# A hybrid attention layer on one core: other order of the beginning, first group's stack rows written and loaded alone, weights loaded later

## The reference, cut to what matters

```python
x = x + attn_a(layernorm(x))     # differential attention, 16 heads, two softmax maps per head, head size 4
x = x + ffn(layernorm(x))        # 64 experts of 128x64 and 64x128, top 8 chosen per token, plus a shared expert
x = x + attn_b(layernorm(x))     # attention over sums, 16 heads
x = x + ffn(layernorm(x))

# attn_a, x is (2, 1024, 128) float32
qkv = x @ w_qkv.T
q = q.reshape(B, N, 16, 2, 4); k likewise; v = v.reshape(B, N, 16, 8)
a1, a2 = softmax(q1 k1^T / 2) v, softmax(q2 k2^T / 2) v
o = a1 - lam * a2                # then RMS norm per head, weight, projection
```

## Time and profile before

| | |
|---|---|
| median of 3 runs | 1106.67 us (1105.13 to 1108.87) |
| profiled execution | 1106.26 us, its span 1104.3 us |
| PE busy | 1006.7 us (91%) |
| DVE busy | 958.2 us (87%) |
| ACT busy | 891.8 us (81%) |
| POOL busy | 520.5 us (47%) |
| chain that ended last | DVE 58%, PE 25%, ACT 6%, issue 5%, DMA 5% |

### The profile page before, as it was taken

The page is one execution under the profiler, slowest core; times in us unless marked ns, Lnnn a source line. Parts: engine busy times, 40 slices in busy tenths (PEclk is TensorE's granted clock), DMA queues, the critical chain, the costliest instruction groups (busy, mean ns, idle before and its releaser), DMA issues.

```text
span 1104.3 us, 21657 instructions
## 1 busy us (share of the span) xinstructions
PE 1006.7 (91%) x8016; PEld 516.2 (47%) x8016; DVE 958.2 (87%) x1170; ACT 891.8 (81%) x1466; POOL 520.5 (47%) x909
## 2 busy tenths in 40 slices
PE   6389999999999999999999989998899899989998
PEld 3022222222222222222222337776678777867886
DVE  7799999999999999999999747888767977777675
ACT  5179999999999999999999977766676776678775
POOL 3353546455645564556455665354325542443331
PEclk9579999999999999999999999999999999999999
DMA  8901110111011101110110037665467466857774
GB/s 283 302 27 41 52 50 16 37 51 50 13 40 51 50 15 38 52 50 16 37 52 21 4 67 186 154 150 126 117 175 189 118 174 154 195 130 174 189 196 103
DMA packets 80472, 108.91 MB, mean 99 GB/s; under 512 B 23536, under 2 KB 33520, under 8 KB 80368
## 3 DMA queue, kind: packets, MB, share of 16 engines
q1 hardware_dynamic: 66336, 100.98, 34.7%
q10 hardware_dynamic: 14032, 6.55, 2.3%
HBM read 95.57 MB, written 11.93 MB: 97 GB/s over the span
## 4 chain that ended last, share of the span: by engine, by line
DVE 58%; PE 25%; ACT 6%; issue 5%; DMA 5%; SPq 1%; POOL 0%; ACTq 0%; DVEq 0%
DVE NEGMAX L1058 47%; PE PS L1450 6%; PE PS L1452 6%; PE PS L1451 6%; DVE HF L1099 3%; DMA GATE<-gate_d 3%; DVE XC L1005 2%; PE PS L1352 2%; DVE HL L1107 2%; ACT PS L948 2%; ACT PR L853 1%; PE PS L1325 1%; ACT L948 1%; DVE ln_st L993 1%; ACT HH L941 1%
## 5 line engine op out<-in xcount | busy, mean ns | idle before, releaser
L1058 DVE TENSOR_REDUCE NEGMAX<-PS 128x1 f32<-128x1024 f32 x512 | 584.8, 1210 | 10.0 <-PE PS L1288 9.4
L853 ACT ACTIVATE PR<-PS 128x512 f32<-128x512 f32 x1024 | 539.0, 601 | 37.4 <-PE PS L1325 24.9
L1352 PE MATMUL PS<-PR,VG 128*32 128x256 f32 (+1 forms) x3840 | 322.1, 407 | 17.1 <-ACT PR L853 1.8
L1325 PE MATMUL PS<-QB,KB 32*128 32x512 bf16 x1024 | 260.5, 388 | 3.2 <-DMA QB<-shift_d 1.9
L1099 DVE TENSOR_TENSOR HF<-PS,GATE 128x1024 f32<-128x1024 f32 x128 | 156.0, 1221 | 89.9 <-ACT PS L948 82.8
L1288 PE MATMUL PS<-KA,QA 32*128 32x512 bf16 x1024 | 204.8, 398 | 30.7 <-DVE NEGMAX L1058 22.6
L948 ACT ACTIVATE PS<-PS 128x1024 f32<-128x1024 f32 x128 | 129.2, 1009 | 89.5 <-PE PS L1452 88.4
L1325 PEld LDWEIGHTS PS<-QB,KB 32*128 32x128 bf16 x1024 | 75.1, 91 | 239.7 <-ACT PR L853 138.5
L765 POOL TENSOR_TENSOR HL<-HF,HH 128x1024 fp32r<-128x1024 f32 (+1 forms) x48 | 108.9, 2268 | 160.7 <-ACT HH L941 160.4
L941 ACT ACTIVATE HH<-HF 128x1024 fp32r<-128x1024 f32 (+1 forms) x136 | 139.7, 1028 | 35.0 <-DVE HF L1099 34.1
L1352 PEld LDWEIGHTS PS<-PR,VG 128*32 128x32 f32 x3840 | 76.5, 108 | 130.8 <-issue 64.6
(11 more groups left out here) (186 smaller groups left out, 985.8 us busy)
## 6 DMA issues: line engine op xcount, KB each, us to landing
GATE<-gate_d SPq DMA_DIRECT2D x256, 256.0 KB, 4.1
QA<-q_stack SPq DMA_DIRECT2D x64, 128.0 KB, 2.6
QB<-q_stack SPq DMA_DIRECT2D x16, 256.0 KB, 3.0
KB<-k_stack SPq DMA_DIRECT2D x16, 256.0 KB, 3.0
KA<-k_stack SPq DMA_DIRECT2D x60, 64.0 KB, 2.4
q_stack<-PARTS SPq DMA_DIRECT2D x12, 256.0 KB, 4.3
k_stack<-PARTS SPq DMA_DIRECT2D x12, 256.0 KB, 4.0
RAWU<-in_L_ffn_W_up_dram ACTq DMA_DIRECT2D x4, 512.0 KB, 10.8
```

The source lines that it names most:

```text
L853: nc.scalar.activation(PR[:, s % PRING, r, :], PS[:, SCORE_BANK[n], :], ACT.Exp, scale=SCALE_A).then_inc(p_ready, 1)
L1058: nc.vector.tensor_reduce(NEGMAX[:, hs % 2, col:col + 1], PS[:, e:e + 2, :].rearrange("p b n -> p (b n)"), axis=AX_X, op=ALU.max, negate=T ...
L1325: mm(PS[:, SCORE_BANK[n], :], KB[strip, u, mt * P:(mt + 1) * P], QB[strip, u, half * BANK:(half + 1) * BANK], start=True, stop=True).then_ ...
L1352: last = mm(PS[STRIP * r:STRIP * (r + 1), 7, cols], VG[:, u, mt, r // 2, :], PR[:, s % PRING, r, cols], start=mt == 0, stop=mt == TB - 1 a ...
```

## The change

What it does:

- **Loads.** `WQKV` and `WPRJ` are issued by ACT, so the four loads of X stand at SP's start alone. The fills come ahead of `CENT` and `WB`. The small mixed loads (`LAM`, `BPROJ`, `SUBW`, `BO`, `EBIAS`) move behind the writes of batch element 0, `RAWSU` and `RAWSD` behind all stack writes and behind the loads of group 1. `RAWD` and `RAWU` are issued by ACT behind its last copy of chunk 3.
- **Stacks.** In DRAM the slot is now the inner index, and one transfer writes a part into all its slots: six transfers instead of twelve. The rows of group 0 are written first, by six transfers of their own (one by ACT), then loaded; groups 1 to 7 follow.
- **Order.** Chunks 0 and 1 go through transposition, products and splitting ahead of chunks 2 and 3. `R1` has four places instead of two. POOL makes the low parts of chunks 0, 2 and 3. The values of chunks 2 and 3 and the `centT` item are computed by PE between maximum items 1 and 2 (`late_values`).
- **Warm matmuls.** PE does 10 transposes of `ident` into an unused bank ahead of the weights and 9 behind them.
- **POOL.** `shift_parts(0)` comes ahead of the low part of `RAWD`; the low parts of the other weights move behind `shift_parts(1)`, the addition of `BPROJ` to X behind the work of half-group 3. POOL, not DVE, computes the lambda sums.

```diff
+FIRST_WRITES = 16 * 2 * 4
+STACK_WRITES = (16 * 2 * 3, 16 * 2 * 4)
...
@@ SP
-                if c == 0:
-                    sp.dma_start(WQKV[:], w_qkv.rearrange("(j p) c -> p j c", p=P)).then_inc(ld_w, 16)
-                    sp.dma_start(WPRJ[:], w_proj).then_inc(ld_w, 16)
...
+            def write_parts(queue, j, part, g0, g1, there):
+
+                stack, slots = ((q_stack, Q_SLOTS), (k_stack, K_SLOTS))[j]
+                b, lo, n = g0 // GPB, R * HD_A * (g0 % GPB), R * HD_A * (g1 - g0)
+                src = PARTS[lo:lo + n, part, j, b * SEQ:(b + 1) * SEQ]
+                places = [c for c, a in enumerate(slots) if a == part]
+                step = places[1] - places[0] if len(places) > 1 else 1
+                rows = stack[g0:g1].rearrange("g r d c n -> (g r d) c n")[:, places[0]:places[-1] + 1:step, :]
+                queue.dma_start(rows, src.unsqueeze(1).to_broadcast([n, len(places), SEQ])).then_inc(there, 16)
...
+            sp.wait_ge(st_first, FIRST_WRITES)
+            load_queries(0, 0, 0, qa_first)
+            load_queries(0, 0, 1, qa_ld[0])
+            load_keys(0, 0, 1, qa_ld[0])
+            load_strips(q_stack, QB, 0, 0, sh_w)
+            load_strips(k_stack, KB, 0, 0, kb_ld[0])
+            for part in range(3):
+                for j in range(2):
+                    write_parts(sp, j, part, 1, GPB, st_w[0])
+            fill_shift_rows(1, st_w[1])
...
+            for part, (made, n) in enumerate(((qk_hi, 2 * NCH), (qk_mid, 2 * NCH), (qk_lo_pool, 6))):
+                sp.wait_ge(made, n)
+                for j in range(2):
+                    write_parts(sp, j, part, GPB, NG, st_w[1])
+            sp.wait_ge(st_w[0], STACK_WRITES[0])
+            load_max(1, 1)
+            sp.wait_ge(const_ok, 3)
             sp.dma_start(RAWSU[:, 0:F], ws_up).then_inc(ld_exp, 16)
             sp.dma_start(RAWSD[0:F, :], ws_down).then_inc(ld_exp, 16)
...
@@ ACT
+            values(0)
+            values(1)
+            transposed(2)
+            act.wait_ge(st_first, FIRST_WRITES)
+            for h in range(2):
+                act.dma_start(KA[2 * STRIP * h:2 * STRIP * (h + 1), 0, 0, :],
+                              k_stack[0, 0:2, :, :, h * BANK:(h + 1) * BANK].rearrange("r d c n -> (r d c) n")).then_inc(qa_first, 16)
+            high_part(0, 2)
+            transposed(3)
...
@@ DVE
+            for c in range(2, NCH):
+                rest(0, c)
+                rest(1, c)
...
@@ PE
+            def warm(times):
+
+                for _ in range(times):
+                    nc.tensor.transpose(PS[:, 7, 0:P], ident[:], ident[:])
...
             for s in range(-LEAD, NQ):
+                if s == 1 - LEAD:
+                    late_values()
```

More of the change, by code:

```diff
@@ L135, in ring_order, with a_bank @@
     return {n: i for i, n in enumerate(names)}
-A_ITEM = ring_order(["wT"] + [("xT", c) for c in range(NCH)] + [("va", c) for c in range(NCH)] + ["centT"])
+A_ITEM = ring_order(["wT", ("xT", 0), ("xT", 1), ("va", 0), ("va", 1), ("xT", 2), ("xT", 3), ("va", 2), ("va", 3), "centT"])
+def a_bank(n):
+    late = A_ITEM["va", 2]
+    return n % 4 if n < late else 4 + n - late
 D_ITEM = ring_order([("qk", j, c) for c in range(NCH) for j in range(2)])
@@ new lines, in _, with load_strips, load_queries @@
+            sp.wait_ge(qk_lo, 1)
+            write_parts(sp, 0, 2, 0, 1, st_first)
+            def load_strips(stack, tile, u, g, there):
+                sp.dma_start(tile[:, u, :], stack[g].rearrange("r d c n -> (r d c) n")).then_inc(there, 16)
+            def load_queries(u, g, rp, there):
+                for h in range(2):
+                    strips = slice(2 * STRIP * h, 2 * STRIP * (h + 1))
+                    sp.dma_start(QA[strips, u, rp, :], q_stack[g, 2 * rp:2 * rp + 2].rearrange("r d c n -> (r d c) n")).then_inc(there, 16)
@@ new lines, in load_keys, with load_max @@
+            def load_keys(u, g, rp, there):
+                for h in range(2):
+                    strips = slice(2 * STRIP * h, 2 * STRIP * (h + 1))
+                    sp.dma_start(KA[strips, u, rp, :],
+                                 k_stack[g, 2 * rp:2 * rp + 2, :, :, h * BANK:(h + 1) * BANK].rearrange("r d c n -> (r d c) n")).then_inc(there, 16)
+            def load_max(u, g):
+                for rp in range(R // 2):
+                    load_queries(u, g, rp, qa_ld[u])
+                    load_keys(u, g, rp, qa_ld[u])
@@ L722, in _ @@
                     heads_norm(hs - 2)
+                if hs == 1:
+                    low_weights(1, WUL, RAWU, WUH)
+                    for n, (dst, src, hi) in enumerate(((WSUL, RAWSU, WSUH), (WSDL, RAWSD, WSDH))):
+                        low_weights(n + 2, dst, src, hi)
+                if hs == 3:
+                    pool.wait_ge(ln_xn, NCH)
+                    nc.gpsimd.tensor_tensor(X[:], X[:], BPROJ[:].unsqueeze(1).to_broadcast([P, NT, DIM]), op=ALU.add).then_inc(xb_ok, 1)
                 if hs == 2 * NG - 3:
@@ new lines, in _ @@
+            transposed(0)
+            high_part(0, 0)
+            transposed(1)
+            high_part(1, 0)
+            middle_part(0, 0)
+            high_part(0, 1)
+            middle_part(1, 0)
+            high_part(1, 1)
+            middle_part(0, 1)
+            middle_part(1, 1)
+            act.wait_ge(qk_lo_pool, 2)
+            act.wait_ge(qk_lo, 2)
+            low_keys = k_stack[0].rearrange("r d c n -> (r d) c n")[:, K_SLOTS.index(2), :]
+            act.dma_start(low_keys, PARTS[0:R * HD_A, 2, 1, 0:SEQ]).then_inc(st_first, 16)
@@ L792, in _ @@
+            middle_part(1, 2)
+            high_part(1, 3)
+            middle_part(0, 3)
+            middle_part(1, 3)
+            values(2)
+            values(3)
+            n = A_ITEM["centT"]
+            act.wait_ge(a_full, n + 1)
+            nc.scalar.activation(CT[:], PS[:, a_bank(n), 0:E], ACT.Copy)
+            nc.scalar.activation(WVT[:], PS[:, a_bank(n), E:E + DIM], ACT.Copy).then_inc(a_free, 1)
             act.dma_start(RAWD[:].rearrange("p (j d) -> p j d", d=DIM),
                           w_down.rearrange("(j e) f d -> (e f) j d", e=2)).then_inc(ld_down, 16)
-            def load_up(part):
+            for part in range(4):
@@ L1041, in _ @@
                                   H16[:].unsqueeze(2).to_broadcast([P, HEADS_B, HD_B])).then_inc(blk_ok, 1)
+            for c in range(2):
+                dve.wait_ge(ld_x[c], 16)
+                stats(("a", c))
+            norm(("a", 0))
+            norm(("a", 1))
+            dve.wait_ge(ld_x[2], 16)
+            stats(("a", 2))
+            rest(0, 0)
+            dve.wait_ge(ld_x[3], 16)
+            stats(("a", 3))
+            rest(1, 0)
+            rest(0, 1)
+            rest(1, 1)
+            low_part(0, 1)
+            low_part(1, 1)
+            norm(("a", 2))
+            norm(("a", 3))
+            for c in range(2, NCH):
+                rest(0, c)
+                rest(1, c)
             def slot(it):
@@ L1223, in ring @@
                 n = items[key]
-                if n >= 4:
+                if n >= 4 and (items is D_ITEM or a_bank(n) < 4):
                     pe.wait_ge(free, n - 3)
-                put((0 if items is A_ITEM else 4) + n % 4).then_inc(full, 1)
+                put(a_bank(n) if items is A_ITEM else 4 + n % 4).then_inc(full, 1)
             def transposes(tiles):
```

250 lines of the change are left out of this document (118 added, 132 removed).

## The result

| | before | after |
|---|---|---|
| median | 1106.67 us (1105.13 to 1108.87) | 1139.24 us (1137.18 to 1140.44) |
| ratio | | 1.0291, 95% interval 1.0270 to 1.0312 |
| span of the profiled execution | 1104.3 us | 1138.2 us |
| first exponential | 61.88 | 74.35 |
| copy of the 2nd and of the 32nd shift tile (`SHT`) by DVE | 77.14 and 628.28 | 88.37 and 661.79 |

The change makes the kernel 2.9% slower. The sign was forecast, the size was not: 1110.4 us, with 1114 as the upper end. A fourth run of the kernel before took 1464.94 us and is left out of its median.

What follows compares the result with a forecast made beforehand. DVE's maximum pass was taken as the bound, with full DMA queues holding the first exponential. Its 7.3 us earlier start goes into waiting; item 28 4.2 to 4.8 us later, less 0.6, gives +3.9 on 1106.26: 1110.4 us, range 1104 to 1114.

Steps and rivals of the forecast that it cites:

- From there on: From first exponential into the loop: item 28 at 71.9 to 72.5, 4.2 to 4.8 us later; 0.6 back from PE's clock.
- A loop bound like this moves as a whole: DVE's maximum pass, 512 items of 1.21 us: starting it d earlier or later moves the end by d.
- The first ladder: Steps up to the maximum pass: first NEGMAX at 27.4, not 35.58; after a 0.9 us gap, item 24 7.3 us earlier.
- the drain: Transfers ahead of the first exponential: 12.5 MB left at 27.4, done at 62.6 (bounds 60 and 68.8); first exponential at 66.7.
- Splits 4.1: ACT between drain and first exponential: WUH and the small splits take 4.1 us, as before.
- item 28: Maximum item whose matmuls start 5.2 to 5.8 us after the first exponential, so at 71.9 to 72.5.
- The last step of the sum: Adding +3.9 us to the profiled execution of 1106.26, 0.4 below the median of 1106.67, to forecast 1110.4 us.
- Edits at nothing: Fewer transfers, POOL's moved low parts and X + BPROJ, lambda sums on POOL: no cost, lambda sums late only if small loads are.
- Rival D: Stack writes: narrow or scattered ones are slower, first group lands 2.7 us later, total 1113 or more; chance 0.08.
- B: Rival at the start: queues drain faster, near 59, first exponential near 63, total about 1107.5; chance 0.20.
- C: Rival at the start: only the maximum pass counts, its 7.3 us come through whole, total 1099.4; chance 0.10.
- A: The forecast itself: the drain holds the first exponential, range 1107.5 to 1114; chance 0.62.

Runs made afterwards that it cites:

- b3: a4 without the 19 warm transposes: 1117.1 us, ratio 1.0098.
- a3: The changed kernel with RAWD issued behind ACT's first copy again and its split ahead of RAWU's issue: 1138.8 us, ratio 1.0298.
- d1: Kernel before with RAWD directly ahead of RAWU, RAWSU and RAWSD behind group 1, RAWD's low part behind POOL's first shift parts: 1120.9 us, ratio 1.0138.
- b1: a4 with RAWD issued early, WDH ahead of RAWU's issue, and RAWSU, RAWSD and the nine small loads behind WB: 1110.4 us, ratio 1.0035.
- c2: b1 with the old row order (adjacent shift rows, each slot written by its own transfer): 1110.7 us, ratio 1.0028.
- d2: Kernel before with probe loads on SP into an unread scratch tile, rows adjacent or spaced, to time the issue: one execution, 1140.35 us.
- a4: The changed kernel with the shift rows of all four sub-heads by one load of 16 rows, 8 partitions apart: 1115.6 us, ratio 1.0089.

## Where the prediction was right and where it failed

- **"From there on": failed, and this is most of the error.** "A loop bound like this moves as a whole" took it for granted that nothing per half-group had changed. The 10.0 us of waiting said only that the cover was enough for the old issues. The new pattern of the shift rows in `QB` was priced nowhere, not even at nothing with a cover named. The runs showed in its place 0.63 us instead of 0.27 per issue, four per half-group, and 0.74 us per half-group: 22.3 of the 29 us by which the forecast was short.
- **The first ladder: right in direction, half of the gain.** First `NEGMAX` at 31.37 and not 27.4, with a gap of 0.67 behind it, so item 3 is 3.5 us earlier than before and not 7.3. The last first-group write was issued at 21.18, not at 18.8: the first product of chunk 0 took 2.07 us and the three behind it 4.23, where I had put 1 us for each. The rests of chunks 2 and 3 then took until 31.4. The warm transposes did not change the first product (b3).
- **Bytes right, rate of the drain mis-sized, 7.7 us short.** From 27.4 to 69.6 us, when `RAWU`'s last packets ran, 13.0 MB moved (12.5 forecast), at 308 GB/s in the mean. That is the 302 of the earlier trace rows, which the prediction held as its lower bound with an end at 68.8; for the sum it took 355 to 400 from the best short windows. Such windows are there (365 GB/s from 40 to 45, 369 from 55 to 60), but in the second one `RAWU` got only 0.25 MB, and its rest came late and slowly: all queues moved 258 GB/s from 60 to 65 us and 191 from 65 to 70. ACT also came to the issue of `RAWD` at 34.12, not 30.4. `WUH` started at 70.33, not 62.6. The forecast had the shift rows at the same time as the weights, and so they were: the first score at 72.72 says that `WUH` at 62.6 would not have brought the first exponential to 66.7 by itself. The wait for `RAWSU` and `RAWSD`, which I had put first, is real too: it holds `WUH` as soon as `RAWD` is out of the way (a3).
- **Splits 4.1, item 28 behind the first exponential 5.2 to 5.8: right.** `WUH` to first exponential is 4.02. Only `WDH`, which ACT could not make while it was issuing, was missing: it ended at 70. The last step of the sum is loose (1106.26 + 3.9 is 1110.2, 1106.67 + 3.9 is 1110.6), which changes nothing.
- **Edits at nothing: POOL right, with a value.** The moved low parts cost nothing, and d1 shows the 6.9 us wait that they would have cost in their old place. But the small loads, of which I had said that the lambda sums are late only if they are, made POOL wait and delayed the first shift tile by 2.2 us, which b1 removed. POOL of the changed kernel:

```profile
53.03 0.48 POOL L688 TENSOR_TENSOR lam_p<-LAM 128x4 f32<-128x4 f32 x2 [17.47 <-DMA EBIAS<-L_ffn_expert_biases_dram]
```

- **Rival D: not borne out.** The last write of the first group, from 16 partitions, was issued at 21.18, and its loads went out at 24.03: 2.85 us at most, no more than the 2.94 of the earlier trace rows. The Trainium skill ("SBUF — State Buffer", "Door 1: The DMA port swizzle") gives 104 GB/s for so few partitions. This last write is only 32 KB, and all six, 0.39 MB, had 5.4 us from the first issue; so the trace doesn't speak against the rule, it shows that it cost nothing here.
- **The rivals.** B and C fell with `WUH` at 70.33. A's mechanism, the drain that holds the first exponential, is what happened at the start, with a first exponential at 74.35 and not 66.7. None of the four had a loss in the loop, so no chance stood on 1139.

## What to carry to other kernels

Of an edit that changes a layout, price every transfer that touches the layout, in the loop above all: its issue time as well as its bytes. A loop's small waits show how much cover the present costs have left, not that new ones would be covered; here 1.6 us of issue per half-group became 0.74 us of time, 30 times. And before a start is moved, list every line that meets in the first dependent instruction: here an edit that moved one line alone gained nothing (a3, c2), and the two lines had to move together (d3).

## What the hardware did that I had not expected

- SP needs 0.27 us to issue a load into three adjacent partitions and 0.63 us if they are 2, 4 or 8 apart (d2). Each set was issued only when the one ahead had landed.
- Two queues do not share by bytes or evenly, and the share swings. Beside one-slot writes `RAWU` moved 0.62 MB in 5 us in the earlier trace rows and 0.73 in c2, but within the first of these windows 0.02 MB from 42 to 43 us and 0.25 from 43 to 44. In five windows of b1 and c2 in which q1 moved 1.4 to 1.5 MB, it got 0.23 to 0.40, with either row order. In packets it is one of q1 to 3.9 of q10 in the earlier trace rows, and one to 1.15 in the changed kernel from 55 to 60. The Trainium skill ("DMA: Bandwidth & Descriptors", "Queues, rings and completion order") says that an engine takes turns between queues and drains a whole packet of several descriptors in each. No run here shows turns, and what sets the share stays open.
- 256-byte lines move fewer bytes for the same share: 0.63 MB in 5 us at a share of 0.60, nearly alone (a4, 65 to 70 us), where the writes of the earlier trace rows moved 1.15 MB at 0.60.
- In the first ladder the record says full clock (1.00 from 8 to 16 us) while a product takes 2.07 us; a product takes about 1 us in the earlier trace rows (1.98 for two), where PE has run for a while.
